# A fused vision-transformer kernel: GpSimd's remainder subtraction moved between two scatters, ScalarE's rounding moved ahead of a norm, and a long subtraction halved

## The reference

```python
# x: 128 images of 3 x 224 x 224; 64 patches of 28 x 28 x 3 each (2352 numbers), one class token: 65 tokens of 128
tokens = (concatenate([cls, patches @ W.T + b])) * pos_embed
h = tokens
h = h + attention(layernorm(h))          # keys, queries, values; causal; softmax over the query axis
h = h + top2_of_32_experts(layernorm(h)) # sigmoid gates; relu(x @ keys[e]) @ values[e]
h = h + abs(norm(cumsum(h') - shifted(h')) * decayed_sum(h'))   # h' = layernorm(h)
h = h + top2_of_16_experts(layernorm(h)) # softmax gates; gelu(x @ w1 + b1) @ w2 + b2
```

## Time and profile before

| | |
|---|---|
| median of 3 runs | 1117.15 us (1115.98 to 1121.53) |
| span of the profiled execution | 1116.9 us |
| busy: TensorE, VectorE | 927.8 us (83%), 861.5 us (77%) |
| busy: GpSimd, ScalarE | 674.1 us (60%), 500.2 us (45%) |

### The profile page before, as it was taken

One profiled execution on the slowest core, in us unless ns is written; L12 is line 12 of the kernel. 1 busy time (PEld: TensorE's weight loads), 2 busy tenths in 40 slices (PEclk: granted clock), 3 DMA queues, 4 the chain that ended last, 5 costly groups with the idle time before them and its releaser, 6 DMA issues.

```text
span 1116.9 us, 21766 instructions
## 1 busy us (share of the span) xinstructions
PE 927.8 (83%) x6072; PEld 782.8 (70%) x6072; DVE 861.5 (77%) x3342; ACT 500.2 (45%) x1340; POOL 674.1 (60%) x622
## 2 busy tenths in 40 slices
PE   6999999999999985567676876677629999999992
PEld 2576667777776654456665865667629999999992
DVE  0488988889888985656677897799867777888883
ACT  1355555554445442111112553666625555666651
POOL 1026666676666643576777667677776555555552
PEclk9999999999999986577887887677758999999997
DMA  9856665566665014377789973665385889889886
GB/s 374 347 199 206 223 222 193 198 206 231 215 230 204 25 40 122 103 200 201 210 224 306 302 226 107 224 195 173 122 284 179 259 277 279 289 284 334 292 299 229
DMA packets 118665, 246.58 MB, mean 221 GB/s; under 512 B 20914, under 2 KB 85936, under 8 KB 112400
## 3 DMA queue, kind: packets, MB, share of 16 engines
q1 hardware_dynamic: 77440, 191.26, 51.6%
q0 software_dynamic: 18592, 34.68, 9.2%
q10 hardware_dynamic: 22512, 19.25, 5.8%
HBM read 201.68 MB, written 45.43 MB: 221 GB/s over the span
## 4 chain that ended last, share of the span: by engine, by line
PE 43%; DVE 25%; issue 9%; SPq 8%; DMA 7%; ACT 5%; ACTq 1%; POOL 1%; DVEq 0%; POOLq 0%
PE ps L968 10%; PE ps L946 7%; PE ps L747 4%; PE ps L814 3%; SPq L606 3%; PE ps L798 3%; SPq L604 2%; SPq L597 2%; DVE idx L1611 2%; ACT x_hi L1129 2%; PE ps L771 2%; PE ps L740 2%; PE ps L786 2%; PE ps L923 2%; DMA results_L<-xin 2%
## 5 line engine op out<-in xcount | busy, mean ns | idle before, releaser
L2090 POOL DMA_INDIRECT lists_L<-rows,slots x250 | 281.2, 1125 | 177.2 <-issue 174.5
L2118 POOL DMA_INDIRECT results_L<-xin x145 | 144.0, 993 | 110.0 <-DVE xin L1890 80.8
L2118 POOL DMA_INDIRECT results_L<-xin,place x146 | 144.4, 989 | 60.4 <-issue 39.3
L747 PE MATMUL ps<-xin,w_emb 128*128 128x512 f32 x292 | 138.2, 611 | 9.7 <-DMA w_emb<-in_w_main 8.5
L968 PE MATMUL ps<-xin,QK 128*128 128x128 f32 x838 | 116.4, 291 | 1.9 <-DVE xin L1890 1.7
L968 PEld LDWEIGHTS ps<-xin,QK 128*128 128x128 f32 x838 | 108.3, 205 | 3.5 <-issue 3.5
L1290 ACT ACTIVATE QK<-ps,xin 128x256 f32<-128x256 f32 x164 | 64.2, 474 | 79.7 <-PE ps L946 79.7
L2099 POOL TENSOR_TENSOR x_lo<-xin,x_hi 128x2048 fp32r<-128x2048 f32 x13 | 60.2, 4630 | 63.8 <-ACT x_hi L1137 63.5
L747 PEld LDWEIGHTS ps<-xin,w_emb 128*128 128x128 f32 x292 | 53.0, 195 | 59.1 <-issue 48.5
L923 PE MATMUL ps<-ident,xin 128*128 128x128 f32 x291 | 66.0, 310 | 32.6 <-DMA xin<-lists_L 30.7
L968 PE MATMUL ps<-xin,UH 128*128 128x128 f32 x648 | 91.0, 287 | 2.5 <-DVE xin L1890 2.2
(11 more groups left out here) (312 smaller groups left out, 2435.2 us busy)
## 6 DMA issues: line engine op xcount, KB each, us to landing
xin<-in_x_main SPq DMA_DIRECT2D x48, 1536.0 KB, 6.8
xin<-in_w_L SPq DMA_DIRECT2D x81, 578.0 KB
xin<-in_w_L SPq DMA_DIRECT2D x98, 128.0 KB
xin<-lists_L SPq DMA_DIRECT2D x64, 132.0 KB
xin<-in_w_L ACTq DMA_DIRECT2D x65, 128.0 KB
x_hi<-results_L SPq DMA_DIRECT2D x13, 640.0 KB, 6.3
xin<-in_difference SPq DMA_DIRECT2D x13, 640.0 KB, 5.0
xin<-in_distance SPq DMA_DIRECT2D x13, 640.0 KB
```

The costliest lines, as they stand in the source:

```text
L747: mm = pe.matmul(psE[h], w_emb[:, k, :], xin[h][c][:, n, :], start=(k == 0), stop=False, skip_group_check=True)
L2090: pool.indirect_dma_start(out=lists[l.name], out_offset=bass.IndirectOffsetOnAxis(ap=slots_of(l, g, h)[:, t, k:k + 1], axis=0), in_=buf[:, ...
L2118: pool.indirect_dma_start(out=results[l.name], out_offset=bass.IndirectOffsetOnAxis(ap=where, axis=0), in_=yblk[u][:, q, :], in_offset=Non ...
```

## The change

On GpSimd `low0` of the first group runs ahead of everything, and from then on a group's scatters are sent as eight, then `low0` for the group four ahead, then the last two. On ScalarE `high0` moves from behind `r1_rows1` to ahead of `guessB`, and `high` is cut into two halves of three tiles, with the copy `XT` of `a2` between them. On VectorE the subtraction of `low` is two instructions of 1536 columns; the first waits for the first half of the rounding, the second for the second half and the rest.

```diff
-            def high(g, h, j):
+            def high_of(h, first, end):
+                return act.activation(x_hi[:, first:end, :].rearrange("p k n -> p (k n)"),
+                                      xin[h][SPLIT][:, first:end, :].rearrange("p k n -> p (k n)"), ACT.Copy)
+
+            def high_begin(g, h, j):
 
                 act.wait_ge(chunk_in[h][SPLIT], 32 * (j + 1))
...
-                act.activation(x_hi[:, :, :].rearrange("p k n -> p (k n)"),
-                               xin[h][SPLIT][:, :, :].rearrange("p k n -> p (k n)"), ACT.Copy)
+                high_of(h, 0, KC // 2).then_inc(x_hi_ready, 1)
+
+            def high_end(g, h, j):
+
+                high_of(h, KC // 2, KC)
                 act.activation(rest[half[h], :], xrest[h][:, :], ACT.Copy).then_inc(x_hi_ready, 1)
...
                     guess(LNA, g + 1, statsA, logA, guessA)
+                if FIRST <= g + 3 < GROUPS:
+                    high0(g + 3, 1 - h, (g + 3) // 2)
                 guessB(L0, g)
                 if ahead_e:
-                    high(g + 2, h, j + 1)
+                    high_begin(g + 2, h, j + 1)
                 if ahead:
                     a2(g + 1, o, jo)
+                if ahead_e:
+                    high_end(g + 2, h, j + 1)
+                if ahead:
                     a3(g + 1, o, jo)
                 r1_x2T(L0, g, h, j)
                 r1_rows1(L0, g, h, j)
-                if FIRST <= g + 3 < GROUPS:
-                    high0(g + 3, 1 - h, (g + 3) // 2)
...
-                dve.wait_ge(x_hi_ready, g)
-                x = xin[h][SPLIT][:, :, :].rearrange("p k n -> p (k n)")
+                dve.wait_ge(x_hi_ready, 2 * g - 1)
...
-                dve.tensor_tensor(x_lo[:, :, :].rearrange("p k n -> p (k n)"), x,
-                                  x_hi[:, :, :].rearrange("p k n -> p (k n)").bitcast(F32), ALU.subtract)
+                for part_, (first, end) in enumerate(((0, KC // 2), (KC // 2, KC))):
+                    if part_ == 1:
+                        dve.wait_ge(x_hi_ready, 2 * g)
+                    dve.tensor_tensor(x_lo[:, first:end, :].rearrange("p k n -> p (k n)"),
+                                      xin[h][SPLIT][:, first:end, :].rearrange("p k n -> p (k n)"),
+                                      x_hi[:, first:end, :].rearrange("p k n -> p (k n)").bitcast(F32), ALU.subtract)
...
-            def low_and_send(g, h, j):
-                if g + 3 < GROUPS:
-                    low0(g + 3, 1 - h)
-                send(L0, g, h)
-
-            pairs(pool, low_and_send)
+            def send_and_low(g, h, j):
+                send(L0, g, h, 0, 8)
+                if g + 4 < GROUPS:
+                    low0(g + 4, h)
+                send(L0, g, h, 8, TILES * TOP)
+
+            low0(FIRST, FIRST % 2)
+            pairs(pool, send_and_low)
```

More of the change, by code:

```diff
@@ L1254, in _ @@
             guess(LNA, 0, statsA, logA, guessA)
-            high(1, 1, 0)
+            high_begin(1, 1, 0)
+            high_end(1, 1, 0)
             for f in (a2, a3, a4):
```

## The result

The change made the kernel slower: 1131.77 us (1126.65 to 1132.19, median of 4 runs) against 1117.39 us before (1115.98 to 1121.53, 4 runs), a ratio of 1.0105 with a 95% interval of 1.0078 to 1.0133. The forecast of 1110.7 us and its range of 1107 to 1118 are both missed.

What follows compares the result with a forecast made beforehand. TensorE was taken to bound the front stage, busy 24.83 of 25.13 us in a step. Gains of 4.1 + 1.2 + 1.6 less 0.5 in step 0 gave 6.4 us off, 1110.7 us as median, range 1107 to 1118.

Steps and rivals of the forecast that it cites:

- The step that failed first: VectorE's second half, released at about 167.2, is ready before the first ends at 167.26; splitting the subtraction costs nothing.
- The slower rival: `low0` takes the port between the halves of VectorE's subtraction; 2.4 us in each of 12 steps, 1146 us; chance 0.12.
- its point of decision: For `low0` between the halves: whether VectorE's next operation is ready when the first half ends.
- The argument against it: Against `low0` between the halves: in the earlier trace the held scatter did not get in between `x_lo` and `rest`.
- The second step that failed: Step 0: the first `low0` starts earlier and delays VectorE's `x_lo` by 2 us; cost taken as 0.5 us.
- The upper bound (2.6): Step 0: the most it could lose, if the `rows` group ahead is held by `low0` too.
- the mechanism of the gain: `low0` ends ahead of `oh`, which falls from 2.45 to 0.56 us; `pick`, `b1` and, through early `XT`, Q come sooner.
- the second rival: `low0` holds off VectorE's `V`, from 170.06 to 174.4; 2.4 us a step, 1146 us; chance 0.05.
- The no-change rival: The counted gaps are mostly TensorE's pipeline tails, so little is gained: 1114 to 1116 us; chance 0.23.
- 4.1 + 1.2 + 1.6: Gains: 4.1 us ahead of `b1` in 12 steps, 1.2 from `r3`'s wait in step 12, 1.6 from earlier Q in 6.
- the gap ahead of `b1`: TensorE between `tiles(0, 2)` and `b1`: 0.48 us in one step, 0.66 in the next, falling to 0.23; mean gain 0.34.

Runs made afterwards that it cites:

- the late release: VectorE's second half is released only after ScalarE's `rest`, as in the changed kernel: 1131.77 us against 1117.39 before the change.
- the first `high0` late: Changed kernel with the first `high0` back behind `rows1`, in step 0 only: 1127.84 us, ratio 1.0070 to the kernel before the change.
- both repairs: Changed kernel with the second half released right after its own copy and step 0's `high0` back behind `rows1`: 1108.49 us, ratio 0.9903.
- early release: Changed kernel with VectorE's second half released right after its own copy, no longer after ScalarE's `rest`: 1115.17 us, ratio 0.9959.
- the kernel with one piece: Kernel with the early release and late first `high0`, but VectorE's long subtraction in one piece again: 1154.32 us, ratio 1.0331.

## Why the prediction was wrong

**The step that failed first** is the margin of VectorE's second half: "The first half starts at 165.5 and ends at 167.26; the second needs `rest`, 167.2 ... nothing." The margin of 0.1 us was sized well: in steps 1 to 12 it came out between 0.02 and 0.27. That it is enough as long as it is positive is what failed. In the five kernels with the late release the scatter comes in between the halves at margins up to 0.16 us, and does not from 0.16 us on. A tenth of a microsecond on either engine decides: in step 7 ScalarE's `rest` begins 9.31 us after `atok`, in step 4 9.20; in step 6 9.19 as well, but there VectorE began its first half 0.13 us earlier.

**The slower rival** was this one, with a chance of 0.12, and its point of decision was right for the border between the halves: whether VectorE's next operation is ready in time. Its place was off by one border. The scatter came in between the halves; `low0` came behind the second, ahead of a `rest` that needed no further signal. The price was off too: 2.8 us over a short step, 2.0 over a step of before, in 7 steps, instead of 2.4 in 12. The argument against it, "that the held scatter did not get in between `x_lo` and `rest`", was a misreading of the earlier trace rows. The scatter ends at 169.73, 0.16 us after `rest`, but 0.87 us after `x_lo` (165.51 + 3.35 = 168.86), and 0.87 us is what a scatter still needs once it is let in. So it did get in there, and the trace of before already had GpSimd at that border in each of steps 1 to 13; it cost nothing that shows (`rest` took 0.69), since what stood there was a scatter. A subtraction costs 4.2 to 4.3 us (`rest` at 4.90 and 5.03). The rule of the Trainium skill's page "SBUF — State Buffer", section "Who interferes with whom", that whoever issues first has the shared pair for its whole instruction, agrees with these traces where `low0` waits ahead of `rest`. It does not account for the short steps: in step 4 the scatter began at 177.70, ahead of the border between the halves (178.60), and the second half still went first.

**The second step that failed** is step 0: "I take 0.5 us, since no one-input group of the trace is seen held." It cost 6.5 us, 31.49 instead of 25.02; with the first `high0` late step 0 takes 24.79 us. The trace of before had no `ntok` or `rows` beside a `low0`, so there was nothing to be seen held; that was taken for a finding. The upper bound (2.6) counted `low0` mainly against `x_lo`; it was `ntok`, on which TensorE waits (4.24 us), that it held. That section of the Trainium skill also says that a `tensor_scalar` can enter a mode with two ports and then contends with GpSimd; the trace shows the contention, 5.56 against 1.37 us, but not the mode.

**Right** were the mechanism of the gain, and that `V` is not held: in the short steps it runs under `low0` in its usual 1.22 us, so the second rival falls. `oh` is free, 0.56; `b1` follows by 0.23; Q follows its tile by 1.73 or 1.74 us in steps 1 to 13; the later ninth and tenth scatter, the early `high0` ahead of `guessB`, and the 15 more instructions cost nothing that shows. The no-change rival is out: with both repairs the same moves save 11.1 us.

**Mis-sized** is the gain: 4.1 + 1.2 + 1.6 = 6.9 us over steps 1 to 12. With both repairs these take 294.1 us instead of 305.2, 11.1 less: 0.8 in an ordinary step where the sum had 0.48, and 1.9 in step 12 where it had 1.7 at most. (The sum has 0.82 us for 1024 columns of ScalarE's copy; 2.75 - 1.91 is 0.84. A half took 1.47, so nothing hangs on it.) A part is the gap ahead of `b1`: the 0.48 us of step 3 was taken for every other step, and most of these had 0.54 to 0.58. In step 4 of the changed kernel `b1` starts 22.11 us after `atok`, in the same step before 22.75: 0.4 of it between `r3` and `b1`, as the sum had it for such a step, and 0.1 each by the Q and K matmuls and ahead of `r3`, which the sum did not have. Nor are the terms separate. `XT` in time gives nothing with `oh` held (25.4 a step, though Q follows its tile by 1.74), and `oh` need not be quite free: at 1.4 us, with `low0` earlier by a slipped scatter, the steps are 24.5 too. `oh` free without `XT` in time was not tried by itself.

**Open** stays why the limit is 0.16 us: the traces show where it lies, not what it is made of. Open is why an early release closes the border between the halves while the one ahead of `rest` stays open with no signal to wait for. Open is also why VectorE's whole subtraction is held in four steps of the kernel with one piece: its row begins 0.16 to 0.22 us before that of `low0`, and yet it is `low0` that has the port. How many long steps the executions without a profile have is not known; one of the changed kernel's four took 5 us less than the others.

## What to carry to other kernels

When two engines take turns at a shared port, they wait for each other on more than semaphores (`rest`, `ntok` and `oh` here), and a border between two back-to-back instructions is an opening. Cutting a long instruction makes one more. Here that one closed when the second piece was released early enough (0.15 us before the first ended was too little, 0.17 enough), so look at its release, and give it a signal of its own. The border ahead of `rest` stayed open in every kernel; there it mattered only what stood next in the other engine's queue. Before reading a held instruction as one that was kept out, compare its end with every border ahead of it, and with how long it needs once it is let in. And when an instruction is moved to a place where the trace never had it, "never seen held" means nothing unless the trace has the two side by side.

## What the chip showed that was not expected

- GpSimd gets in between two VectorE operations that follow each other within 0.02 us (the long subtraction and `rest`): a waiting subtraction makes the second take 5.03 us instead of 0.69, a waiting scatter leaves it at 0.69. Between the two halves a scatter gets in only when the second is released no more than about 0.16 us before the first ends.
- A scatter that is held ends 0.85 to 0.89 us after the end of the VectorE subtraction that held it (0.99 us undisturbed).
- `tensor_scalar` with one fp32 input in SBUF is held by a GpSimd subtraction (5.56 us for five instead of 1.37); operations that read PSUM (`V`, `Sm`, `lg`) and the reductions `smax` and `top` ran beside it unheld.
- A difference of 0.1 us on ScalarE or VectorE, from one step to the next, decides over 2.7 us on TensorE.
